# FFN weight tiles transposed by DMA instead of TensorE, and a new order of work at both ends of an adaLN-FFN kernel

## The reference

```
y  = einsum('bij,bkj->bik', x, weight[adapter_ids])      # f32, 1024 x 1024 for each sequence
h  = layernorm(y) * gamma + beta
h  = fake_quant(h) @ fake_quant(w1).T + b1               # quantised by row: s = max|row| / 127
g  = gelu(h)                                             # exact, not the tanh form
out = x + fake_quant(g) @ fake_quant(w3).T + b3
```

## Time and profile before

| | us |
|---|---|
| median of 3 runs | 372.67 |
| lowest, highest | 368.39, 375.36 |
| the profiled execution | 374.43 |
| its span, first to last instruction | 372.5 |

### The profile page before, as it was taken

How to read it: one execution, slowest core, us unless ns; L and a number is a source line. 1 busy time by engine, 2 the same in 40 slices (tenths; PEclk the granted TensorE clock), 3 DMA queues, 4 the chain that set the end, 5 groups by cost and what they waited for, 6 DMA issues and landing times.

```text
span 372.5 us, 5769 instructions
## 1 busy us (share of the span) xinstructions
PE 341.4 (92%) x1854; PEld 235.9 (63%) x1880; DVE 285.5 (77%) x344; ACT 227.1 (61%) x232; POOL 263.4 (71%) x164
## 2 busy tenths in 40 slices
PE   6898899996976999999999999999899989999885
PEld 6787788754763666666665666566566666674442
DVE  1459698886946777798778886888779687999866
ACT  2433476854888647773777658755777477625651
POOL 1402259841998579995999599968997699946831
PEclk9999999999899999999999999999999999999989
DMA  6999998695950899539971999099925990150014
GB/s 186 352 347 352 410 280 164 147 246 117 241 99 0 199 276 218 100 119 294 221 154 63 299 223 203 0 268 244 220 56 158 288 229 0 58 171 1 0 55 172
DMA packets 46203, 67.35 MB, mean 181 GB/s; under 512 B 2918, under 2 KB 37734, under 8 KB 46186
## 3 DMA queue, kind: packets, MB, share of 16 engines
q1 hardware_dynamic: 46186, 67.14, 68.8%
HBM read 58.74 MB, written 8.39 MB: 180 GB/s over the span
## 4 chain that ended last, share of the span: by engine, by line
POOL 41%; issue 22%; DMA 13%; DVE 11%; PE 7%; SPq 3%; ACT 2%; POOLq 0%; DVEq 0%
POOL y L458 8%; POOL x_res L474 7%; POOL o L466 6%; POOL y L460 5%; DMA x_res<-in_L_ffn_w 5%; POOL a L478 4%; POOL x_lo L483 4%; POOL o L469 3%; DMA w_scale_row<-in_L_ffn_w 3%; PE t_ps L1134 2%; DMA h_r<-in_L_cond_weight 2%; DVE x_nat L917 2%; DMA x_t<-in_L_ffn_b 2%; DVE wq_max L861 2%; DMA w_nat<-in_L_cond_weight 2%
## 5 line engine op out<-in xcount | busy, mean ns | idle before, releaser
L1080 PE MATMUL a_ps<-w_hi,x_hi 128*128 128x512 f32 x256 | 107.5, 420 | 2.4 <-DVE w_lo L794 1.2
L1082 PE MATMUL a_ps<-w_hi,x_lo 128*128 128x512 f32 x256 | 100.8, 394 | 0.0
L1081 PE MATMUL a_ps<-w_lo,x_hi 128*128 128x512 f32 x256 | 100.7, 393 | 0.0
L1134 PE MATMUL f_ps<-w_q,q_t 128*128 128x512 bf16 x377 | 88.1, 379 | 9.7 <-ACT q_t L627 8.2
L1134 PEld LDWEIGHTS f_ps<-w_q,q_t 128*128 128x128 bf16 x400 | 37.1, 98 | 57.5 <-ACT q_t L627 12.5
L803 DVE STREAM_TRANSPOSE t_ps<-w_nat 128x1024 f32<-128x1024 f32 x48 | 57.5, 1238 | 11.7 <-DMA w_nat<-in_L_cond_weight 11.5
L809 DVE TENSOR_TENSOR w_lo<-t_ps,w_hi 128x1024 fp32r<-128x1024 f32 x48 | 57.2, 1219 | 8.9 <-ACT w_hi L574 8.7
L574 ACT ACTIVATE w_hi<-t_ps 128x1024 fp32r<-128x1024 f32 x48 | 49.0, 1023 | 21.9 <-DVE t_ps L803 21.1
L1080 PEld LDWEIGHTS a_ps<-w_hi,x_hi 128*128 128x128 f32 x256 | 48.5, 189 | 15.7 <-ACT y L589 3.2
L1082 PEld LDWEIGHTS a_ps<-w_hi,x_lo 128*128 128x128 f32 x256 | 48.5, 189 | 10.7
L1081 PEld LDWEIGHTS a_ps<-w_lo,x_hi 128*128 128x128 f32 x256 | 48.6, 190 | 9.0
(11 more groups left out here) (151 smaller groups left out, 503.1 us busy)
## 6 DMA issues: line engine op xcount, KB each, us to landing
w_nat<-in_L_cond_weight SPq DMA_DIRECT2D x96, 256.0 KB, 6.5
x_res<-in_x SPq DMA_DIRECT2D x7, 1024.0 KB, 6.3
out<-o SPq DMA_DIRECT2D x14, 512.0 KB, 3.1
x_nat<-in_x SPq DMA_DIRECT2D x24, 256.0 KB, 9.9
w_nat<-in_L_cond_weight SPq DMA_DIRECT2D x10, 512.0 KB, 8.9
w_q<-in_L_ffn_w SPq DMA_DIRECT2D x4, 512.0 KB, 7.9
h_r<-in_L_cond_weight SPq DMA_DIRECT2D x4, 512.0 KB, 6.7
w_scale_row<-in_L_ffn_w SPq DMA_DIRECT2D x3, 512.0 KB, 10.3
```

The lines of the kernel that those rows point to most:

```text
L1080: pe.matmul(ps, hi, w_hi[:, u, c], start=begin, stop=False)
L1081: pe.matmul(ps, hi, w_lo[:, u, c], start=False, stop=False)
L1082: last = pe.matmul(ps, lo, w_hi[:, u, c], start=False, stop=end)
L1134: last = pe.matmul(ps[:, half, :], q[:, c, :], w[:, c, half_of(half)], start=c == 0, stop=c == CB - 1)
```

## The change

Every FFN weight tile is still loaded, scaled and rounded as before. Then, in place of TensorE's eight transposes and ScalarE's copy out of PSUM, ScalarE subtracts the magic number and writes the integers as bf16 into the first half of the same buffer (`packed`), and its queue sends one transposing DMA per tile from there to `w_q` (`transpose_prep`). All waits on the old counters become waits on one semaphore for each tile. `scale_row` waits for PSUM to be free by other counters.

The orders of all five lists in the first three sequences are written anew. SyncE sends six of the weight tiles ahead of sequence 0's last unit. Sequence 0's `piece(0, 2, 1)` moves ahead of transpose_first(10); `transpose_g(0, 0)` ahead of `piece(2, 1, 1)`.

In the last sequence `residual_last` moves from VectorE to GpSimd, behind VectorE's two bias halves; GpSimd's second residual of sequence 6 moves behind these too; ScalarE's take of sequence 6's second tile moves ahead of the GELU halves; and GpSimd no longer makes `minus_mean` and `shift` for it (the end doesn't use them). The diff is shown with eight columns of indent taken off; cut from it: declarations, the constant `minus_magic`, the split of `residual` into tiles, and parts of the lists with the same kinds of steps.

```diff
@@ -303,7 +308,8 @@
     def load_residual(b):
         if isinstance(b, int) and b == 0:
-            sp.wait_ge(wq_transposed, 11)
+            sp.wait_ge(wq_ready[9], 16)
+            sp.wait_ge(wq_ready[10], 16)
         else:
             sp.wait_ge(out_ready, TT * b)
         src = x[bass.ds(b, 1)].rearrange("o (t p) d -> p (o t) d", p=P)
@@ -347,7 +353,7 @@
             elif i in (11, 12):
                 sp.wait_ge(first_transposed, first_piece(0, 1) + 1)
             elif i == 13:
-                sp.wait_ge(wq_transposed, RT)
+                sp.wait_ge(wq_ready[7], 16)
             elif i >= 14:
                 sp.wait_ge(h_rounded, i - 13)
             src = (w1, w3)[i // RT][(i % RT) * P:(i % RT + 1) * P, :]
@@ -382,28 +388,24 @@
     load_first_unit(1)
     load_rows()
     load_first_unit(2)
-    load_prep((2, 4))
+    load_prep((0, 6, 5, 1, 3, 2))
+    load_first_unit(3, (1,))
+    load_first_unit(3, (0,))
     load_rows_of_w((0,))
-    load_prep((0,))
-    load_first_unit(3, (1,))
-    load_prep((1,))
-    load_first_unit(3, (0,))
-    load_prep((3, 5))
+    load_prep((8, 7, 4))
     load_rows_of_w((1,))
-    load_prep((6,))
-    load_rows_of_w((2, 5))
+    load_prep((10, 9))
+    load_rows_of_w((3, 2, 6, 4))
     load_second_x()
+    load_rows_of_w((5,))
     load_prep((11,))
-    load_rows_of_w((3,))
-    load_prep((7, 8, 9))
-    load_rows_of_w((4, 6, 7))
-    load_prep((12, 10))
+    load_x(2)
+    load_prep((12,))
+    load_rows_of_w((7,))
+    load_unit(2, 0)
+    load_prep((13, 14, 15))
     load_unit(2, 1)
-    load_x(2)
-    load_unit(2, 0)
-    load_prep((15, 14))
     load_unit(2, 2)
-    load_prep((13,))
     load_unit(2, 3)
     load_residual(0)
     load_x(3)
@@ -437,19 +439,20 @@
 def _(pool):
     def normalisers(n, tiles):
-        mean, variance = (mean_var[:, tiles, k:k + 1].rearrange("p t o -> p (t o)") for k in (0, 1))
+        variance = mean_var[:, tiles, 1:2].rearrange("p t o -> p (t o)")
         pool.tensor_tensor(var_eps[:, tiles], variance, eps[:, tiles], ALU.add).then_inc(var_eps_ready, 1)
-        pool.tensor_tensor(minus_mean[:, tiles], mean, minus_one[:, tiles], ALU.mult).then_inc(minus_mean_ready, 1)
         pool.wait_ge(var_eps_ready, n + 1)
         pool.tensor_tensor(rstd[:, tiles], var_eps[:, tiles], minus_half[:, tiles], ALU.pow).then_inc(rstd_ready, 1)
-        pool.wait_ge(minus_mean_ready, n + 1)
-        pool.wait_ge(rstd_ready, n + 1)
-        pool.tensor_tensor(shift[:, tiles], minus_mean[:, tiles], rstd[:, tiles], ALU.mult).then_inc(shift_ready, 1)
     def normalisers_of(b):
         pool.wait_ge(mean_var_ready, TT * (b + 1))
         wait_past(pool, normed, TT * b)
+        pool.tensor_tensor(minus_mean[:], mean_var[:, :, 0:1].rearrange("p t o -> p (t o)"), minus_one[:],
+                           ALU.mult).then_inc(minus_mean_ready, 1)
         normalisers(b, slice(0, TT))
+        pool.wait_ge(minus_mean_ready, b + 1)
+        pool.wait_ge(rstd_ready, b + 1)
+        pool.tensor_tensor(shift[:], minus_mean[:], rstd[:], ALU.mult).then_inc(shift_ready, 1)
     def scale_and_shift(f, t):
         n = TT * f + t + 1
...
@@ -518,20 +522,18 @@
         pool.partition_broadcast(rows[:, k], rows_1[k]).then_inc(rows_ready, 1)
     round_prep((0, 1, 2, 3, 4, 5, 6))
     normalisers_of(0)
-    round_prep((7,))
+    round_prep((7, 8))
     scale_and_shift(0, 0)
-    round_prep((8,))
     scale_and_shift(0, 1)
-    round_prep((9, 10, 11, 12))
+    round_prep((9, 10, 11, 12, 13, 14))
     low_x(2, 0)
     add_b1(0, 0)
+    round_prep((15,))
+    low_x(2, 1)
+    normalisers_of(1)
     add_b1(0, 1)
-    round_prep((13,))
-    low_x(2, 1)
-    round_prep((14, 15))
-    normalisers_of(1)
+    scale_and_shift(1, 0)
     residual(0)
-    scale_and_shift(1, 0)
     scale_and_shift(1, 1)
...
@@ -540,6 +542,15 @@
         period(p)
     f = LAST - 1
+    def residual_last(t):
+        pool.tensor_tensor(x_last[:, t], x_last[:, t], b3_row, ALU.add).then_inc(x_last_ready, 1)
+    def finish_last(t):
+        pool.wait_ge(last_o_scaled, KH * (t + 1))
+        pool.wait_ge(x_b3_ready, TT * f + t + 1)
+        pool.tensor_tensor(o[:, t, :], o[:, t, :], x_res[:, t, :], ALU.add).then_inc(out_ready, 1)
     pool.wait_ge(mean_var_ready, TT * LAST + 1)
     pool.wait_ge(normed, TT * LAST)
     normalisers(LAST, slice(0, 1))
@@ -549,11 +560,15 @@
     add_b1(f, 1)
     pool.wait_ge(ffn1_scaled, KH * (TT * LAST + 1))
     pool.tensor_tensor(a_last[:, 0], a_last[:, 0], b1_row, ALU.add).then_inc(ffn1_biased, 1)
-    residual(f)
-    for t in range(TT):
-        pool.wait_ge(last_o_scaled, KH * (t + 1))
-        pool.wait_ge(x_b3_ready, TT * f + t + 1)
-        pool.tensor_tensor(o[:, t, :], o[:, t, :], x_res[:, t, :], ALU.add).then_inc(out_ready, 1)
+    residual(f, (0,))
+    pool.wait_ge(last_half_biased, KH)
+    pool.wait_ge(x_last_loaded, 16)
+    residual_last(0)
+    residual(f, (1,))
+    finish_last(0)
+    residual_last(1)
+    finish_last(1)
 @block.scalar
...
@@ -632,15 +647,23 @@
         act.activation(o[:, t, :].rearrange("p (h k) -> p h k", k=BANK), ps, ACT.Identity,
                        scale=g_scale[:, t:t + 1]).then_inc(ffn2_scaled, 1)
-    def take_prep(tiles):
+    def transpose_prep(tiles):
         for i in tiles:
-            act.wait_ge(wq_transposed, i + 1)
-            rows_of_tile = slice((i % RT) * P, (i % RT + 1) * P)
-            act.activation(w_q[i // RT][:, :, rows_of_tile], transposed(f_ps[:, i % 2], I16), ACT.Copy
-                           ).then_inc(wq_ready, 1)
+            act.wait_ge(wq_rounded, i + 1)
+            act.activation(packed(prep_slot[i]), prep_slot[i], ACT.Identity, bias=minus_magic[:]).then_inc(wq_packed, 1)
+        for i in tiles:
+            if i == RT:
+                for j in range(4):
+                    act.wait_ge(wq_ready[j], 16)
+            act.wait_ge(wq_packed, i + 1)
+            act.dma_start_transpose(w_q[i // RT][:, :, (i % RT) * P:(i % RT + 1) * P], packed(prep_slot[i])
+                                    ).then_inc(wq_ready[i], 16)
     def take_scale_row(n):
         act.wait_ge(scale_row_done, n + 1)
+        act.wait_ge(wq_ready[(6, 13)[n]], 16)
         act.activation(w_scale_row[:, n, :].rearrange("p (h k) -> p h k", k=BANK), f_ps[:], ACT.Copy
                        ).then_inc(scale_row_ready, 1)
@@ -698,11 +721,11 @@
         round_g(f, 1)
         act.wait_ge(ffn1_biased, TT * LAST + 1)
         act.activation(a_last[:, 0], a_last[:, 0], ACT.Gelu).then_inc(g_ready, 1)
+        take(g_transposed, TT * f + 2, t_ps[:, 0, 0], q_t[:, 1], g_t_ready)
         for half in range(KH):
             part = a_last[:, 1, half_of(half)]
             act.wait_ge(last_half_biased, half + 1)
             act.activation(part, part, ACT.Gelu).then_inc(last_half_gelu, 1)
-        take(g_transposed, TT * f + 2, t_ps[:, 0, 0], q_t[:, 1], g_t_ready)
         act.wait_ge(g_inv_ready, TT * LAST + 1)
         act.activation(a_last[:, 0], a_last[:, 0], ACT.Identity, scale=g_inv[:, TT:TT + 1], bias=magic[:]
                        ).then_inc(g_rounded, 1)
@@ -725,58 +748,55 @@
     copy_y(0, 0)
     split_first(8)
     split_first(9)
+    transpose_prep((0, 1, 2, 3))
     split_first(10)
     split_first(11)
     split_first(12)
-    take_prep((0,))
     split_first(13)
+    copy_y(0, 1)
     split_first(14)
...
+    split_first(17)
+    transpose_prep((7,))
     normalise(0, 1)
-    split_first(17)
-    take_prep((6,))
     split_first(18)
-    take_prep((7,))
     split_first(19)
-    take_prep((8,))
+    transpose_prep((8,))
+    take_scale_row(0)
     copy_y(1, 0)
     round_h(0, 0)
-    take_scale_row(0)
     round_h(0, 1)
+    transpose_prep((9, 10, 11))
     split_w(2, 0, 0)
     take_h(0)
     split_w(2, 0, 1)
     split_x(2, 0)
-    both(2, 1)
+    transpose_prep((12, 13))
+    split_w(2, 1, 0)
+    transpose_prep((14,))
+    copy_y(1, 1)
+    split_x(2, 1)
+    split_w(2, 1, 1)
     gelu(0, 0)
-    split_w(2, 2, 0)
-    copy_y(1, 1)
-    take_prep((9,))
-    split_x(2, 1)
-    take_prep((10,))
+    transpose_prep((15,))
+    normalise(1, 0)
     round_g(0, 0)
-    take_prep((11,))
...
@@ -870,6 +890,8 @@
     def rescale1(f, t, ps=f_ps, dst=a, col=None):
         if isinstance(f, int) and f == 0:
             dve.wait_ge(scale_row_ready, 1)
+            if t == 0:
+                dve.wait_ge(wq_ready[8], 16)
         col = t if col is None else col
         for half in range(KH):
             dve.wait_ge(ffn1_done, KH * (TT * f + t) + half + 1)
@@ -912,10 +934,6 @@
             dve.bn_aggr(mean_var[:, t, :], stats[:, t].rearrange("p h s -> p (h s)")
                         ).then_inc(mean_var_ready, 1)
-        def residual_last(t):
-            dve.wait_ge(x_last_loaded, 16)
-            dve.tensor_tensor(x_last[:, t], x_last[:, t], b3_row, ALU.add).then_inc(x_last_ready, 1)
-
         def last_gamma(t):
             dve.wait_ge(mean_var_ready, TT * LAST + t + 1)
```

(71 more changed lines are left out.)

83 lines of the change are left out of this document (40 added, 43 removed).

## The result

The changed kernel takes 401.8 us (median of 4 runs, 399.3 to 406.2), the kernel before 373.3 on the same chip: a ratio of 1.082 (95% interval 1.061 to 1.103). The forecast was 363.5. The profiled execution took 399.3 us; its span is 397.5, 25.0 more than before.

A forecast was written before the change was run, and what follows sets the result against it. Loading was taken to bound the start until 64.59 us, then handing on between engines. Start -4.7 and end -4.5 made -9.2 us, from a median of 372.67 to 363.5; range 359 to 369, chance 0.43.

The forecast's parts named there:

- part 2: ScalarE's cost: 16 issues of transposing DMAs at 0.5 us, 8 us, and packs at 1.24 us against takes of 1.02, +3.5.
- Part 1: TensorE, no longer transposing 16 weight tiles at 0.43 us each, saves 7.0 us, 3.9 of it behind 64.59 us.
- Part 3: DMA engines: each 256 KB transpose takes 0.65 us of all engines, far end 1.3, near end nothing.
- Part 4: First half of the start: transpose_first(19) ends at 66.1 us against 64.6 before, a loss of 1.5 us.
- Part 5: From transpose_first(19) to the loop: 51.2 us against 57.4, so the loop begins at 117.3 instead of 122.0, -4.7 us.
- Part 6: The end, after the loop: the moved take and residuals shorten it by 4.5 us, bounds -2 and -5.5.
- slow transposes: Rival, chance 0.14: transposes go one after another at 6.5 us each, or issues take over 2.0 us; 394 us in total.

The follow-up runs named there:

- experiment 2: The changed kernel with its transposing DMAs replaced by plain copies of the same bytes: 371.69 us (1.006) in long rows, 381.1 us (1.027) in 256-byte pieces.
- experiment 4: The kernel before, old lists, only tiles 9 to 15 by transposing DMA: issued by ScalarE 1.042, by SyncE 1.026, by SyncE with a new end 1.021.
- experiment 3: The changed kernel with its first four transposes issued singly between hi copies: 385.05 us (1.040); with tiles 9 to 11 also single and later: 384.62 (1.041).

## Why the prediction was wrong

The failed step is part 2's price, "I take 0.5, a little above the median as a transfer with more pieces: 8 us". The 16 issues took 45 us: 1.25 the least, 8.9 the most. I had the row that warned, 1.61 us as the highest of SyncE's own issues, and set it aside as "a full queue"; the start is where queues are full, share 1.00. Worse than the size was the form of the cost. I set mean issue time against mean idle time (28.9 us in 88). But four issues in a row are one block, 20.1 us, and the hi copies behind it feed VectorE, PE and through PE the loads. The batch is an item of the diff, and I never walked ScalarE's list behind it.

- **Part 1** (TensorE saves 7.0 us): PE's busy time of both halves fell by 98.1 - 97.1 = 1.0 only, since it ran longer at the low clock (granted 0.85 and 0.90 in the two halves, against 1.00 and 0.97). A saving on PE is worth nothing where it then waits.
- **Part 2, the pack**: 1.14 to 1.16 us against 1.24 taken; right and small.
- **Part 3** (0.65 us a tile, far end 1.3): 1.36 alone, 1.38 beside loads at the kernel's end, 2.2 on average in place. The far end was too near. The rule of the Trainium skill that I weighed there, "Advanced Engine Details and Errata", X-Bar Transpose, by which transposing DMAs run as fast as plain ones, does not hold here: 1.36 us against 0.70 for the same bytes in long rows. The other, "VectorE: DVE Perf Modes", The three transpose paths, held in its sign (DMA dearer than TensorE's 0.43 us), but its blocks do not add up one after another: eight come in 1.36 us, not 10.5.
- **Part 4** (66.1): 83.6. With long-row copies (0.85 us a tile by their queue's share, dearer than the 0.65 of the sum) 62.5, so the walk of the load queue was 3.6 us too late; the orders were not the trouble.
- **Part 5** (loop 51.2 us after it, wait of 2.3 at ffn1(0, 0)): 64.3, and 6.9 at ffn1(0, 0), for the same reason: ScalarE stood 8.3 us behind issues. Behind it ffn2(0, 0) waited 3.48 us for the last tile, which the sum had at nothing, and the wait of 2.3 at ffn1(0, 1) did not come. Even with cheap copies the half took 56.4 us, among the 52.8 to 58.8 of the seven traces with the old lists. So the 4.7 us that the start was to gain rest in part on the base: 121.98 was the highest of seven loop starts, and the wait of 3.13 us that the new lists were to shorten stands in only two of them.
- **Part 6** (-4.5, bounds -2 to -5.5): -1.1 in the trace and 1.002 alone. Right were the removed wait of 2.74 us, the bias half at 0.69, PE's run of 9.7 us from the last-but-one transposes (380.70 to 390.41), and that `rstd` would take `minus_mean`'s wait (1.41 us). Wrong was "GpSimd's last additions end near 364.5, just in time": the check asked when they end, not what they do to VectorE meanwhile. Two of VectorE's last four additions stood beside it whole (2.06 and 2.05 us); in the kernel before, where GpSimd had finished by 364.3, only the first met its last 0.6 us (1.15, then three of 0.69 us).
- **The rivals**: 401.8 is beyond all of them. The nearest was *slow transposes* (394, 0.14), by its second route, issues over 2.0 us (measured 2.8 in the mean). Its first route, tiles landing 6.5 us one after another, is not what happened: six alone came 1.36 apart.

That the transposes are the cause, and not the orders, is shown by experiment 2. That being held on ScalarE is a part of it is shown by experiment 4's move to SyncE (1.042 to 1.026), with seven tiles in the old lists; for the changed kernel it is read from the waits, and experiment 3 fits it. How the loss splits between the hold, the engines' time and the late landing was not separated.

## What to carry to other kernels

A DMA issue on a compute engine's queue is an instruction of that engine with a length of its own; price it by the slowest issue in a trace whose queues are as full, and walk what stands behind it, a batch as one block. Do not replace 0.4 us of TensorE by a transposing DMA where loads fill the queues, and do not trust a mean DMA share of 0.59 to say that they don't. Before you forecast a gain of a few us in one stage, see from a second trace how much that stage varies. When work is moved to GpSimd, ask which VectorE instruction will lie beside it.

## What the hardware showed that was not expected

- An issue to ScalarE's queue took at least 1.25 us for a transpose, 0.60 for 256-byte pieces and 0.47 for 2 KB rows, and up to 10.0 us beside twelve queued loads for a transpose, 9.9 for 256-byte pieces.
- A transposing tile of 256 KB is 1056 packets, and took twice the engines' time of 2 KB rows (1.36 against 0.70 us); under the start's loads 4.5 from 40 to 45 us.
- Loads fell only from 384 to 361 GB/s at the kernel's end while a second queue held four tiles, whose landing went from 3.4 to 10.8 us: there the small transfers were late, not the large ones.
- PE's granted clock was at 0.50 after waits of 16.8 and 6.9 us, and the FFN product behind the second took 6.03 us instead of 3.6.
- VectorE's two-operand addition of 512 columns took 2.06 us beside a GpSimd addition and 0.69 without it; its maximum of two single numbers took 2.04 and 0.16, and ended with GpSimd's instruction.
- The same start, in seven traces, reached the loop between 115.7 and 122.0 us.
